# One running sum for the expert rows of a four-stage sequence kernel, and a closing stage that reads one row per token

## What is computed

```python
logits = x @ gate_w.T                      # 64 experts
topk_w, topk_ids = top_k(softmax(logits), 8)
topk_w = topk_w / topk_w.sum(-1)
# for each of a token's 8 experts e, with weight w:
#   row = (silu(x @ w_gate[e].T) * (x @ w_up[e].T)) @ w_down[e].T * w
y = sum of the token's 8 rows
x = layernorm(x + y)                       # no gain, no bias, eps 1e-5
```

## Time and profile before

| what | value |
|---|---|
| median of three runs | 4667.4 us |
| the profiled execution, its own time | 4671.13 us |
| its span, first to last instruction | 4669.3 us |
| TensorE clock granted, mean over the span | 0.967 of full |
| `experts`, first to last scatter issue | 3847.2 to 4592.4 us |
| `combine`, barrier to end | 4606.5 to 4669.3 us |

### The profile page before, as it was taken

How to read it: one execution, slowest core, us unless ns; L and a number is a source line. 1 busy time by engine, 2 the same in 40 slices (tenths; PEclk the granted TensorE clock), 3 DMA queues, 4 the chain that set the end, 5 groups by cost and what they waited for, 6 DMA issues and landing times. The chain is left out here.

```text
span 4669.3 us, 80269 instructions
## 1 busy us (share of the span) xinstructions
PE 4139.6 (89%) x18254; PEld 2805.0 (60%) x18255; DVE 3336.0 (71%) x7116; ACT 2754.4 (59%) x6638; POOL 2391.4 (51%) x1811
## 2 busy tenths in 40 slices
PE   7888888779999979999999999999986639999997
PEld 2333333236666547777777777777765527777775
DVE  7999999954343668888888888888866543333335
ACT  6777777622212008888888888888863214444442
POOL 5999899720000014444444545444537766566653
PEclk8999999999999989999999999999998869999999
DMA  2222222220100461122121212122136537777777
GB/s 74 77 77 77 77 91 74 97 87 28 65 31 17 150 192 30 41 58 51 38 51 40 59 37 52 38 53 54 41 93 197 186 110 155 158 157 150 160 150 217
DMA packets 344711, 419.03 MB, mean 90 GB/s; under 512 B 68752, under 2 KB 276240, under 8 KB 339104
## 3 DMA queue, kind: packets, MB, share of 16 engines
q1 hardware_dynamic: 243888, 299.10, 21.4%
q0 software_dynamic: 53760, 73.44, 7.6%
q10 hardware_dynamic: 46944, 45.16, 4.7%
HBM read 251.67 MB, written 165.87 MB: 89 GB/s over the span
## 5 line engine op out<-in xcount | busy, mean ns | idle before, releaser
L1811 DVE TENSOR_TENSOR probsT<-ps_t,probsT 128x512 fp32r<-128x512 f32 (+3 forms) x1280 | 781.1, 610 | 120.0 <-ACT probsT L1744 101.6
L1735 ACT ACTIVATE probs<-ps_s,negm 128x512 f32<-128x512 f32 (+3 forms) x1297 | 814.3, 628 | 42.8 <-DVE negm L1794 39.7
L1584 PE MATMUL ps_o<-probsT,vbuf 128*128 128x512 f32 (+3 forms) x2560 | 823.4, 404 | 13.7 <-DVE probsT L1811 6.6
L1561 PE MATMUL ps_s<-kbuf,qbuf 128*128 (+1 forms) x2602 | 769.1, 382 | 69.9 <-ACT probs L1735 44.4
L1744 ACT ACTIVATE probsT<-ps_t 128x512 fp32r<-128x512 f32 (+3 forms) x1280 | 687.7, 537 | 147.1 <-PE ps_t L1572 118.2
L1572 PE MATMUL ps_t<-idn,probs 128*128 128x128 f32 x4352 | 690.8, 274 | 13.6 <-DVE probsT L1811 13.3
L569 POOL TENSOR_TENSOR dBx<-u,b_all 128x1024 f32<-128x1024 f32 x255 | 610.9, 2411 | 93.3 <-DVE h L666 54.5
L1572 PEld LDWEIGHTS ps_t<-idn,probs 128*128 128x128 f32 x4352 | 528.9, 140 | 161.6 <-DVE probsT L1811 31.6
L2612 POOL DMA_INDIRECT sum<-y,place x288 | 448.4, 1557 | 318.8 <-DVE y L2649 309.3
L1561 PEld LDWEIGHTS ps_s<-kbuf,qbuf 128*128 128x128 f32 x2602 | 446.8, 190 | 227.4 <-ACT probs L1735 101.1
L1783 DVE TENSOR_REDUCE least<-ps_s 128x1 f32<-128x512 f32 x781 | 531.5, 681 | 31.1 <-PE ps_s L1561 30.7
(11 more groups left out here) (270 smaller groups left out, 7081.3 us busy)
## 6 DMA issues: line engine op xcount, KB each, us to landing
room_b<-xs ACTq DMA_DIRECT2D x294, 136.0 KB, 2.6
room_a<-q_scr SPq DMA_DIRECT2D x528, 64.0 KB, 1.9
b_all<-b_scr SPq DMA_DIRECT2D x32, 1024.0 KB, 4.7
room_a<-W_guT SPq DMA_DIRECT2D x64, 384.0 KB, 4.2
q_scr<-rot SPq DMA_DIRECT2D x64, 256.0 KB, 2.7
rspread<-r_scr SPq DMA_DIRECT2D x64, 256.0 KB, 3.4
attn_T<-ostage SPq DMA_DIRECT2D x128, 128.0 KB, 2.2
at<-attn_T SPq DMA_DIRECT2D x32, 512.0 KB
```

What stands on the lines that cost most here:

```text
L1561: last = nc.tensor.matmul(ps_s[:, u % RING, 0:w], qbuf[:, BAND * s + j, :], kbuf[:, bass.ds(kslot, 1), part, c * CW:c * CW + w], start=par ...
L1584: last = nc.tensor.matmul(ps_o[:, lo:], vbuf[:, kb, :, :], probsT[:, g % SLOTS, part, lo:], start=kb == 0 and part == 0, stop=kb == BAND * ...
L1735: nc.scalar.activation(probs[:, k, at:at + n, :], ps_s[:, u % RING, 0:n * P], ACT.Exp, bias=negm[:, tile, :], scale=-1.0, accum_out=sums[: ...
L1811: nc.vector.tensor_tensor(probsT[:, g % SLOTS, 1, lo:], ps_t[:, t % 2, lo:], probsT[:, g % SLOTS, 0, lo:].bitcast(F32), ALU.subtract).then ...
```

## The change

`SUMS` goes from 4 to 1, so all expert rows are added to the residual rows, and there is one array. In `experts` nothing else is edited, but the distance in `landed` is `SUMS` as well: it is now one scatter. In `mamba` the three clearing DMAs per chunk go. In `combine` TensorE's part, SP's part, the adds on GpSimd, the Ln and Exp on ScalarE and the Newton step go; all 16 pairs of tiles have a slot (`SUM_SLOTS = 16`; the room is as large as before) and are loaded at the end of `experts`; VectorE reads the loaded rows directly; and GpSimd adds eps and raises to the power, as in `tree_ffn`.

```diff
-        blanked = tally("blanked", 16 * (SUMS + 1))
+        blanked = tally("blanked", 32)
...
-                for total in sums[1:]:
-                    rows = total[c * TC:(c + 1) * TC, :].rearrange("(q p) n -> p q n", p=P)
-                    sp_eng.dma_start(rows, blank[:, :, 0:DM].to_broadcast((P, TC // P, DM))).then_inc(blanked.sem, 16)
...
-SUMS = 4
+SUMS = 1
...
-SUM_SLOTS, SUM_TILES = 4, 2
+SUM_SLOTS, SUM_TILES = 16, 2
...
-        @block.sync
-        def _(sp):
-            for g in range(SUM_SLOTS, PAIRS):
-                sp.wait_ge(summed.sem, summed.at((g - SUM_SLOTS) * SUM_TILES + SUM_TILES - 1))
-                load_sums(sp, rows_in, g, sums)
-
-        @block.tensor
...
-                for a in range(SUMS - 1):
-                    if j == 0 and a == SUMS - 2:
-                        pe.wait_ge(added.sem, added.at(g))
-                    last = nc.tensor.matmul(ps_r[:, t % BANKS, 0:DM], idn, parts[:, g % SUM_SLOTS, a, j * DM:(j + 1) * DM],
-                                            start=a == 0, stop=a == SUMS - 2)
-                last.then_inc(summed.sem, 1)
...
         @block.gpsimd
         def _(pool):
             nc.gpsimd.memset(eps_sb[:, :], EPS).then_inc(eps_set.sem, 1)
-            for g in range(PAIRS):
-                s = g % SUM_SLOTS
-                pool.wait_ge(in_ld[s].sem, in_ld[s].at(g // SUM_SLOTS))
-                nc.gpsimd.tensor_tensor(parts[:, s, SUMS - 2, :], parts[:, s, SUMS - 2, :], parts[:, s, SUMS - 1, :], ALU.add
-                                        ).then_inc(added.sem, 1)
+            nc.gpsimd.memset(nhalf[:, :], -0.5).then_inc(eps_set.sem, 1)
+
+            def inv_std(t):
+                h = t % RING
+                pool.wait_ge(aggr.sem, aggr.at(t))
+                if t >= RING:
+                    pool.wait_ge(o_ready.sem, o_ready.at(t - RING))
+                nc.gpsimd.tensor_tensor(rstd[:, h, :], mv[:, h, 1:2], eps_sb[:, :], ALU.add).then_inc(eps_added.sem, 1)
+                pool.wait_ge(eps_added.sem, eps_added.at(t))
+                nc.gpsimd.tensor_tensor(rstd[:, h, :], rstd[:, h, :], nhalf[:, :], ALU.pow).then_inc(powered.sem, 1)
...
             def add_stats(t):
-                dve.wait_ge(summed.sem, summed.at(t))
-                nc.vector.bn_stats(stats[:, t % RING, :], ps_r[:, t % BANKS, 0:DM]).then_inc(stat.sem, 1)
+                g, j = divmod(t, SUM_TILES)
+                if j == 0:
+                    dve.wait_ge(in_ld[g].sem, in_ld[g].at(0))
+                nc.vector.bn_stats(stats[:, t % RING, :], row_of(t)).then_inc(stat.sem, 1)
...
             def norm_rows(t):
                 h, s = t % RING, t % SLOTS
-                dve.wait_ge(newton.sem, newton.at(t))
+                dve.wait_ge(powered.sem, powered.at(t))
                 if t >= SLOTS:
                     dve.wait_ge(o_out[s].sem, o_out[s].at(t // SLOTS - 1))
-                nc.vector.tensor_scalar(o_sb[:, s, :], ps_r[:, t % BANKS, 0:DM], mv[:, h, 0:1], rstd[:, h, :], ALU.subtract,
+                nc.vector.tensor_scalar(o_sb[:, s, :], row_of(t), mv[:, h, 0:1], rstd[:, h, :], ALU.subtract,
                                         ALU.mult).then_inc(o_ready.sem, 1)
...
             for t in range(NT):
-                if t + 1 < NT:
-                    moments(t + 1)
-                norm_square(t)
                 if t + 2 < NT:
                     add_stats(t + 2)
-                norm_part(t)
-                norm_rstd(t)
                 norm_rows(t)
+                if t + 2 < NT:
+                    moments(t + 2)
```

More of the change, by code:

```diff
@@ L53, in sems, with mamba @@
         return [t.sem for t in self.sig.values()]
-def mamba(nc, x_T, W_inT, conv_w, W_xprojT, W_dtT, b_dt, A_log, D_skip, sel_bc, ident, b_scr, y_scr, xs, sums, tree_front, W_outT):
+def mamba(nc, x_T, W_inT, conv_w, W_xprojT, W_dtT, b_dt, A_log, D_skip, sel_bc, ident, b_scr, y_scr, xs, tree_front, W_outT):
     DI, NST, RANK, TAPS = 512, 16, 16, 4
@@ L2663, in experts, with combine @@
     nc.all_engine_barrier()
-def combine(nc, sums, out, rows_in, idn):
+def combine(nc, out, rows_in):
     SLOTS = 4
-    BANKS = 6
     RING = 4
-    PAIRS = NT // SUM_TILES
     sems = rows_in.sems()
@@ L2685, in combine @@
         mv = sb("mv6", [P, RING, 2])
[L2686 to L2689, removed]
         rstd = sb("rstd6", [P, RING, 1])
         eps_sb = sb("eps6", [P, 1])
-        ps_r = ctx.enter_context(nc.psum_tensor("ps_r6", [P, BANKS, 512], F32))
+        nhalf = sb("nhalf6", [P, 1])
         eps_set = tally("eps_set6")
-        added = tally("added6")
-        summed = tally("summed6")
         stat = tally("stat6")
@@ L2699, in combine @@
         aggr = tally("aggr6")
-        log_done = tally("log6_done")
-        guessed = tally("guessed6")
-        newton = tally("newton6", 3)
+        eps_added = tally("eps_added6")
+        powered = tally("powered6")
         o_ready = tally("o_ready6")
@@ L2756, in _, with row_of @@
             nc.gpsimd.memset(eps_sb[:, :], EPS).then_inc(eps_set.sem, 1)
-            for g in range(PAIRS):
-                s = g % SUM_SLOTS
-                pool.wait_ge(in_ld[s].sem, in_ld[s].at(g // SUM_SLOTS))
-                nc.gpsimd.tensor_tensor(parts[:, s, SUMS - 2, :], parts[:, s, SUMS - 2, :], parts[:, s, SUMS - 1, :], ALU.add
-                                        ).then_inc(added.sem, 1)
+            nc.gpsimd.memset(nhalf[:, :], -0.5).then_inc(eps_set.sem, 1)
[7 more added lines that the diff above has]
+                nc.gpsimd.tensor_tensor(rstd[:, h, :], rstd[:, h, :], nhalf[:, :], ALU.pow).then_inc(powered.sem, 1)
+            pool.wait_ge(eps_set.sem, 2)
+            for t in range(NT):
+                inv_std(t)
         @block.vector
         def _(dve):
+            def row_of(t):
+                g, j = divmod(t, SUM_TILES)
+                return parts[:, g, 0, j * DM:(j + 1) * DM]
             def add_stats(t):
-                dve.wait_ge(summed.sem, summed.at(t))
-                nc.vector.bn_stats(stats[:, t % RING, :], ps_r[:, t % BANKS, 0:DM]).then_inc(stat.sem, 1)
+                g, j = divmod(t, SUM_TILES)
+                if j == 0:
+                    dve.wait_ge(in_ld[g].sem, in_ld[g].at(0))
+                nc.vector.bn_stats(stats[:, t % RING, :], row_of(t)).then_inc(stat.sem, 1)
             def moments(t):
@@ L2772, in moments @@
                 nc.vector.bn_aggr(mv[:, t % RING, :], stats[:, t % RING, :]).then_inc(aggr.sem, 1)
[L2774 to L2789, removed]
             def norm_rows(t):
                 h, s = t % RING, t % SLOTS
-                dve.wait_ge(newton.sem, newton.at(t))
+                dve.wait_ge(powered.sem, powered.at(t))
                 if t >= SLOTS:
                     dve.wait_ge(o_out[s].sem, o_out[s].at(t // SLOTS - 1))
-                nc.vector.tensor_scalar(o_sb[:, s, :], ps_r[:, t % BANKS, 0:DM], mv[:, h, 0:1], rstd[:, h, :], ALU.subtract,
+                nc.vector.tensor_scalar(o_sb[:, s, :], row_of(t), mv[:, h, 0:1], rstd[:, h, :], ALU.subtract,
                                         ALU.mult).then_inc(o_ready.sem, 1)
-            add_stats(0)
-            moments(0)
-            add_stats(1)
+            for t in range(2):
+                add_stats(t)
+                moments(t)
             for t in range(NT):
-                if t + 1 < NT:
-                    moments(t + 1)
-                norm_square(t)
                 if t + 2 < NT:
                     add_stats(t + 2)
-                norm_part(t)
-                norm_rstd(t)
                 norm_rows(t)
+                if t + 2 < NT:
+                    moments(t + 2)
     nc.clear_and_free_semaphores(sems)
@@ L2835, in layers @@
         tree_front = tree_front_of(nc, room_a)
-        mamba(nc, x_T, W_inT, conv_w, W_xprojT, W_dtT, b_dt, A_log, D_skip, sel_bc, ident, b_scr, y_scr, xs, sums, tree_front, W_outT)
+        mamba(nc, x_T, W_inT, conv_w, W_xprojT, W_dtT, b_dt, A_log, D_skip, sel_bc, ident, b_scr, y_scr, xs, tree_front, W_outT)
         room_b = ctx.enter_context(nc.sbuf_tensor("room_b", [P, ROOM], F32))
@@ L2852, in layers @@
         experts(nc, xs, plan_sb, rounds_sb, route_front.buf["idn"], weights_front, rows_front, W_guT, W_downT, sums, rows_in)
-        combine(nc, sums, out, rows_in, route_front.buf["idn"])
+        combine(nc, out, rows_in)
 def constants():
```

4 lines of the change are left out of this document (removed).

## The result

The changed kernel takes 5273.7 us in the median of four runs (5267.0 to 5277.0), the kernel before 4669.1 us in the median of four beside it. The ratio is 1.129, with a 95% interval of 1.127 to 1.130: 13% slower. The forecast was 5329 us, with a range of 5130 to 5470.

What follows compares the result with a forecast made beforehand. TensorE was taken to bound the kernel before, the wait for each scatter's landing after. The profiled 4671.1 + 690 (`experts`) - 28 (`combine`) gave 5333 us, or 5329 us against the median; range 5130 to 5470.

Steps and rivals of the forecast that it cites:

- What bounds it: In `experts`: TensorE sets the pace before; after, GpSimd's wait for the scatter just before sets each step; chance 0.86.
- Landing: In `experts`: time from a scatter's issue start to its data's arrival, taken as 4.1 us (ends 3.6 and 4.4).
- Restart: In `experts`: time from a landing to the next scatter's issue start, taken as 0.9 us (ends 0.3 and 1.2).
- The step: In `experts`: time per scatter, 5.0 us instead of 2.597; over 287 steps +690 us (ends +374 and +862).
- The rule on a DMA's time: For scatters in `experts`: 2.0 us plus bytes over 436 KB per us, so a step of 3.2 us, +173 us; not adopted.
- Closing stage: In `combine`: 62.8 us falls to 34.8, VectorE at 0.95 us per tile, power hidden; -28 us (ends -32 and -16).
- Clearing DMAs: In `mamba`: 24 DMAs of 512 KB go; they lie beside VectorE's work, so 0.
- The turn-backs: In `experts`: the loop's 17 turn-backs, covered by idle time before, may lie open: 0, at most 18 us.
- TensorE at its low clock: Rival in `experts`: TensorE at half clock becomes the bound, 5.2 us a group, 5384 us; chance 0.07.
- The short landing: Rival in `experts`: landings are short when alone, a step of 3.3 us, 4841 us; chance 0.04.
- the faster kernel: Rival: `experts` steps stay under 2.69 us and only the `combine` gain shows, 4639 us; chance of faster 0.01.
- the missing wait: Rival in `experts`: the wait names an older landing, so no step is added, 4639 us; within a chance of 0.01.

Runs made afterwards that it cites:

- the distance alone: The kernel before, with only GpSimd's wait changed to the scatter just before; four arrays, clearing DMAs and old closing stage stay: 5390.4 us, ratio 1.1326.
- the doubled product: The changed kernel, with the gate and up product of every group done twice into the same bank: 5275.7 us.
- the late wait: The changed kernel, with the wait for the landing moved directly ahead of the scatter's issue: 5234.9 us.
- the closing stage alone: The kernel before, four arrays and distance of four, with the changed kernel's `combine` reading only the first array: 4729.6 us, ratio 0.9937.
- halved rows: The changed kernel, each scatter adding only 512 bytes of each row, half of the sums left out: 5127.4 us, ratio 1.098.

## Why the prediction was right

- *What bounds it.* The step of the experts stage was to pass from TensorE to the chain landing and restart. It did, as the distance alone, the doubled product and the late wait show. The sign that I had given for it, idle times ended by the landing, did not come for the reason told above. Nor was TensorE busy about half of the stage: in the stretch shown it was busy 0.76, at a mean clock of 0.85.
- *Landing.* Forecast 4.1 us, measured 3.8. I took the middle between the earlier trace rows. The lone scatter of the earlier trace rows was the right row: with a single scatter in flight and half of the load traffic (83 GB/s instead of 152), the loads beside it cost nothing in the median.
- *Restart.* Forecast 0.9 us, measured 4.795 - 3.8 = 1.0. The 0.78 of the earlier trace rows was the nearest row. The instructions in between took 0.13, as against the guess of 0.1. The error here is 0.1 us upward and the one in the landing 0.3 downward, so they cancel in part.
- *The step.* 5.0 forecast, 4.795 measured, so the term of +690 us is +631; this is the one that was mis-sized. The account against the profiled executions: 5333 forecast, 5267.0 measured, 66 us less, of which 59 are the step, 3 the closing stage and 4 came off before the experts stage. Against the medians it is 55 us, because the profiled execution after lies 6.7 us below its median, where I had taken it to lie 3.7 above, as before.
- *The rule on a DMA's time* ("DMA: Bandwidth & Descriptors" of the Trainium skill, section "Anatomy of one DMA — SWDGE (gpsimd) path") gives an estimate of 2.3 us for 128 KB. It doesn't hold for an adding scatter: no landing of whole rows was under 3.5 us in any run. For the scatters that overwrite it comes near: 2.6 us in the median, 2.4 at the least. The trace decides.
- *Closing stage.* Forecast -28, measured -31.0 and -29.0 alone. The size was right, the pacer wrong. I had VectorE at 0.95 us per tile and GpSimd's 0.82 hidden. Powers are 0.85 us apart (5260.28 and 5261.13), and 31 x 0.10 us is the difference of 3 us. The chain that ended last runs through GpSimd, so GpSimd sets the pace, the sign that I had listed for being wrong here:

```profile
by line: POOL rstd L2719 25.2%; POOL rstd L2717 6.8%; issue 3.0%; POOLq L2670 0.9%; POOLq L2716 0.6%; DVE stats L2735 0.6%; DVE o_sb L2747 0.5%; DVE mv L2740 0.3%; DVEq L2739 0.0%; POOLq L2714 0.0%
```

VectorE is busy 26.27 of the 31.8 us. In this stage the power takes 0.62 us most of the time, where the earlier trace rows showed 0.55.
- *Clearing DMAs.* Forecast 0. The first scatter came 4.3 us earlier in one profiled execution and 0.5 us earlier in the other of the same kernel (3842.9 and 3846.7, before 3847.2), so nothing that stands clear of the differences between executions.
- *The turn-backs,* 0 to 18 us: the steps across the end of a turn are 4.83 us on average, as against 4.795 over all: under 1 us in the sum.
- *Rivals.* TensorE at its low clock was priced at 5.2 us a step. At a mean clock of 0.65 the step was 4.81, so even then it wasn't the bound. In no run did the clock stay at the low level through the whole stage, so a step set by TensorE at 1.2 GHz was never seen. The short landing, the faster kernel and the missing wait are out by the step.

## What to carry to other kernels

Before shortening the distance of a wait, divide: time to landing plus restart, over the distance, against the present step. Here 5.4 / 4 was far under 2.60 and (3.8 + 1.0) / 1 far above. Between them, 5.4 / 3 = 1.8 is under it as well and 5.4 / 2 = 2.7 just above; the first gained 0.3%, and the second lost 0.3% until its restart was made shorter. Then it gained 0.4%. So what doesn't need such a wait belongs ahead of it. The quotient takes the median landing: where it comes close to the present step, the long landings decide. And where one event releases two engines, the profile names the one that came last: count the tiles before believing it.

## What I had not expected of the hardware

Five steps are long, the same ones in the traces before and after and in the runs with one array or a distance of one that still add, and with the closing stage alone: the 60th, 113th, 166th, 219th and 272nd, 53 scatters apart, whether a step takes 2.6 or 4.8 us. The 113th in the timelines before and after:

```profile
4138.02 1.56 POOL L2612 DMA_INDIRECT sum<-y,place  x1 [1.06 <-DVE y L2649]
4142.56 1.55 POOL L2612 DMA_INDIRECT sum<-y,place  x1 [2.98 <-DVE y L2649]
```

```profile
4379.86 1.56 POOL L2609 DMA_INDIRECT sum<-y,place  x1 [3.29 <-DVE y L2646]
4386.67 1.55 POOL L2609 DMA_INDIRECT sum<-y,place  x1 [5.25 <-issue]
```

4.54 us instead of 2.60, and 6.81 instead of 4.8. So it goes by the number of scatters, or by what lies at these places of the program or the input, and not by time. It costs some 0.7 us or 2.0 in turn. Before, GpSimd made it up at once (steps of 1.86 us follow); in the changed kernel nothing makes it up, and the five add some 6 us. The delay is not in the landing: the scatter of 4379.86 landed after 3.8 us as the others do. GpSimd incremented `y_freed` at once, since the `place` that waits for it starts at 4383.93. From there to the next scatter are 2.74 us, where the step of 4298.76 above had 0.80. So the delay lies on GpSimd's side, between the increment and the start of the issue. What happens there stays open. The adding itself costs 0.6 us of issue and another 0.6 us of landing behind it (2.24 as against 1.64 us), more than the 0.5 us that halved rows saved.
